# Three normalised groups turned by DMA as planes of 16-bit halves, and the first products begun by halves

## The reference

```
x = x + 0.5 * ffn(layernorm(x))
x = x + attention(layernorm(x))          # attention normalises again inside, with ln_w and ln_b
x = x + 0.5 * ffn(layernorm(x))

ffn(x):    logits = x @ gate_w.T + gate_b        # 8 experts
           g = top value of softmax(rms(logits) * rms_w / 0.5);  norm_g = g / (g + 1e-6)
           h = gelu(x @ w1[e] + b1[e])           # every expert, 256 hidden each
           out = norm_g * sum over e of (h @ w2[e] + b2[e])
attention: q, k, v = split(ln(x) @ w_qkv)        # 8 heads of 8
           q, k divided by their lengths;  softmax(8 * q @ k.T, causal) @ v;  @ w_out
```

## Time and profile before

| | |
|---|---|
| median of 3 runs | 269.8 us |
| the profiled execution | 269.82 us |
| its span, first to last instruction | 268.1 us |
| granted PE clock, mean | 0.998 |
| PE busy | 258.2 us |
| ACT busy | 217.5 us |
| DVE busy | 216.2 us |
| POOL busy | 80.7 us |

### The profile page before, as it was taken

One profiled execution on the slowest core, in us unless ns is written; L12 is line 12 of the kernel. 1 busy time (PEld: TensorE's weight loads), 2 busy tenths in 40 slices (PEclk: granted clock), 3 DMA queues, 4 the chain that ended last, 5 costly groups with the idle time before them and its releaser, 6 DMA issues.

```text
span 268.1 us, 5428 instructions
## 1 busy us (share of the span) xinstructions
PE 258.2 (96%) x1829; PEld 183.6 (69%) x1829; DVE 216.2 (81%) x590; ACT 217.5 (81%) x344; POOL 80.7 (30%) x175
## 2 busy tenths in 40 slices
PE   7999999999999999979998999999999999999995
PEld 6886878888788786533434433378888887888783
DVE  7999899998898987797378587378889678697784
ACT  2897668859878889999999999987777867859673
POOL 6302104204850482664349545520200000200100
PEclk9999999999999999999999999999999999999999
DMA  5741200001012104101314003300004211210311
GB/s 152 219 123 23 58 1 2 0 1 39 2 34 46 42 2 78 40 1 22 62 39 82 2 4 78 80 1 4 0 8 111 42 39 39 39 34 9 80 39 39
DMA packets 33343, 11.51 MB, mean 43 GB/s; under 512 B 24130, under 2 KB 32548, under 8 KB 33316
## 3 DMA queue, kind: packets, MB, share of 16 engines
q1 hardware_dynamic: 33172, 11.11, 17.7%
q10 hardware_dynamic: 144, 0.07, 0.1%
HBM read 4.88 MB, written 2.62 MB: 28 GB/s over the span
## 4 chain that ended last, share of the span: by engine, by line
PE 73%; DVE 8%; ACT 7%; issue 5%; POOL 4%; DMA 2%; SPq 0%; POOLq 0%; DVEq 0%; ACTq 0%
PE ps L590 10%; PE ps L596 10%; PE ps L608 10%; PE ps L593 10%; PE ps L613 10%; PE ps L611 9%; PE ps L746 5%; ACT probs L937 3%; PE ps L708 2%; PE ps L777 2%; ACT h L924 2%; POOL probs L1533 1%; POOL w_raw L1527 1%; DMA kT<-k_stack 1%; DVE h_lo L1100 1%
## 5 line engine op out<-in xcount | busy, mean ns | idle before, releaser
L924 ACT ACTIVATE h<-ps,cols 128x512 f32<-128x512 f32 x128 | 88.0, 694 | 36.2 <-PE ps L596 32.6
L1100 DVE TENSOR_TENSOR h_lo<-h,h_hi 128x512 fp32r<-128x512 f32 x128 | 88.6, 698 | 19.1 <-ACT h_hi L927 16.7
L937 ACT ACTIVATE probs<-ps 128x1024 f32<-128x1024 f32 (+1 forms) x80 | 65.0, 918 | 1.5 <-PE ps L708 1.4
L590 PE MATMUL ps<-xT_hi,w_hi 128*128 128x512 f32 x128 | 51.5, 402 | 0.0
L608 PE MATMUL ps<-h_hi,w_hi 128*128 128x512 f32 x128 | 50.5, 395 | 0.3 <-ACT yT L949 0.3
L927 ACT ACTIVATE h_hi<-ps,cols 128x512 fp32r<-128x512 f32 x73 | 50.2, 688 | 0.0
L613 PE MATMUL ps<-h_lo,w_hi 128*128 128x512 f32 x128 | 50.2, 392 | 0.0
L596 PE MATMUL ps<-xT_lo,w_hi 128*128 128x512 f32 x128 | 49.9, 390 | 0.0
L593 PE MATMUL ps<-xT_hi,w_lo 128*128 128x512 f32 x128 | 49.9, 390 | 0.0
L611 PE MATMUL ps<-h_hi,w_lo 128*128 128x512 f32 x128 | 49.9, 389 | 0.0
L746 PE MATMUL ps<-probs,v_ones 128*32 128x512 f32 (+4 forms) x384 | 34.2, 458 | 0.9 <-POOL probs L1533 0.6
(11 more groups left out here) (141 smaller groups left out, 273.2 us busy)
## 6 DMA issues: line engine op xcount, KB each, us to landing
w_raw<-in_L_ffn_w SPq DMA_DIRECT2D x8, 256.0 KB, 4.6
turned<-blocks SPq DMA_DIRECT2D x6, 256.0 KB, 2.0
w_raw<-turned SPq DMA_DIRECT2D x24, 64.0 KB, 2.3
w_raw<-v_ones SPq DMA_DIRECT2D x8, 128.0 KB, 2.4
x_sb<-in_L_attn_x SPq DMA_DIRECT2D x3, 256.0 KB, 6.8
out_x<-x_sb SPq DMA_DIRECT2D x3, 256.0 KB, 2.3
w_raw<-o_scaled SPq DMA_DIRECT2D x2, 256.0 KB, 4.3
x_sb<-in_L_attn_x SPq DMA_DIRECT2D x2, 128.0 KB, 2.3
```

Source lines behind the costliest of these rows:

```text
L590: pe.matmul(bank, w1_hi[:, w], xT_hi[:, cols_g], start=True, stop=False)
L924: first = nc.scalar.activation(h[:, slot, :], ps[:, BANK_H + slot, :], ACT.Gelu, bias=bias)
L937: nc.scalar.activation(probs[:, s % P_SLOTS, :, 0:width], ps[:, bank:bank + 2, 0:width], ACT.Exp, scale=SCALE).then_inc(exp_done, 1)
L1100: dve.tensor_tensor(h_lo[:, slot, :], h[:, slot, :], h_hi[:, slot, :].bitcast(f32), ALU.subtract).then_inc(split_done, 1)
```

## The change

Two u16 buffers `planes` and `planes_t` (128 x 2 x 512), `landed` (128 x 512), and semaphores. POOL copies the low and high 16-bit halves of a normalised group into two planes, SP turns both by one DMA transpose, and POOL puts the halves together again. Plane turn 0 is FFN group 3, turn 1 the attention norm of the last group, turn 2 FFN group 4. The PE transposes of these three and the jobs "ln" and "ffn_ln" go. In the start, two of the `keep_busy` calls go and the first pass of the first three chunks is split.

```
+            def turn_planes(n):                                   # SP
+                sp.wait_ge(planes_done, n + 1)
+                sp.dma_start_transpose(planes_t[...], planes[...]).then_inc(planes_in[n], 16)
+                if p == 0:
+                    turn_planes(0)                    # behind group 0's v corners
+                if p == LAST - 1:
+                    sp.wait_ge(xf_done[FFN], GROUPS)
+                    turn_planes(1)                    # ahead of group 2's stacks
+            sp.wait_ge(joined, 1)
+            turn_planes(2)                            # behind all stacks

+            def make_planes(n, kind, normed):                     # POOL
+                pool.wait_ge(xn_done[kind], GROUP_TILES * normed + GROUP_TILES)
+                if n:
+                    pool.wait_ge(planes_in[n - 1], 16)
+                words = xn[:, kind, :, :].rearrange("p t d -> p (t d)")
+                pool.tensor_copy(planes[:, :, :], by_plane(words)).then_inc(planes_done, 1)
+            def join_planes(n, words):
+                pool.wait_ge(planes_in[n], 16)
+                return pool.tensor_copy(by_plane(words), planes_t[:, :, :])
```

POOL's order in the first feed-forward part:

```
+                if layer == 0 and g == 2:
+                    make_planes(0, FFN, LAST)
+                    inverse_lengths(pool, 0, range(1))
+                    ln_twice(1)
...
+                    join_planes(0, xf[:, FFN, :]).then_inc(xf_done[FFN], 1)
+                    gate_root(2)
+                    inverse_lengths(pool, 0, range(1, 3))
+                    unit_vectors(pool, 0)
+                if layer == 0 and last:
+                    low_parts(pool, 0)
+                    inverse_lengths(pool, 1)
+                    ln_twice(2)
+                    unit_vectors(pool, 1)
+                    low_parts(pool, 1)
+                    gate_root(3)
```

and in the attention, behind the masks of the step named:

```
+                if s == 2 * last_quad[1] + 1:         # quad 5
+                    make_planes(1, ATT, LAST)
                 if s == 2 * last_quad[2] + 1:         # quad 12
+                    join_planes(1, landed[:, :]).then_inc(joined, 1)
                     ln_once(GROUPS)
                 if s == 2 * last_quad[5] + 1:         # quad 25
-                    gate_root(GROUPS)
+                    make_planes(2, FFN, GROUPS)
...
+                    join_planes(2, xf[:, FFN, :]).then_inc(xf_done[FFN], 1)
                     ln_once(GROUPS + 1)
                 if s == 2 * last_quad[6] + 1:
+                    gate_root(GROUPS)
```

Who uses them: ACT makes group 3's high part at chunk 10 and DVE its low part at chunk 11 of group 2 (before, 5 and 7). The high parts of the q and k stacks of groups 0 and 1 are made by ACT in chunks 0 and 9 of the last group (before, chunk 9 of group 2 and chunk 8 of the last). Jobs, gate and DVE:

```
-        jobs = [(q1, "ln", LAST), (q1 + 2, "project", (0, 0)), (q1 + 4, "project", (0, 1)),
-                (q1 + 5, "qkv", 0), (q1 + 7, "qkv", 1), (q2 + 3, "ffn_ln", 0),
+        jobs = [(q1 + 2, "project", (0, 0)), (q1 + 4, "project", (0, 1)),
+                (q1 + 5, "qkv", 0), (q1 + 7, "qkv", 1),
-        gate_at = {q2 + 4: GROUPS, quad_steps - 3: GROUPS + 1}
+        gate_at = {q3 + 1: GROUPS, quad_steps - 3: GROUPS + 1}
                 if kind == "qkv":                     # PE, fill
+                    pe.wait_ge(xf_done[ATT], GROUPS)
                 if (kind, arg) == ("project", (0, 1)):            # DVE
                     dve.wait_ge(job_emptied, n + 1)
                     first_stats(GROUPS)
+                    dve.wait_ge(joined, 1)
+                    dve.wait_ge(qkv_mm, LAST)
+                    dve.tensor_scalar(xf[:, ATT, :], landed[:, :], ...).then_inc(xf_done[ATT], 1)
                 if (kind, arg) == ("project", (1, 1)):
                     dve.wait_ge(job_emptied, n + 1)
                     first_stats(GROUPS + 1)
+                    dve.wait_ge(xf_done[FFN], GROUPS + 1)
+                    dve.tensor_copy(xT_hi[:, 0:GROUP], xf[:, FFN, :]).then_inc(early_hi, 1)
...
+                    low_features(dve, GROUPS)
+                    gate_logits(GROUPS, job_bank(n))
```

`gate_shift` and `gate_weight` of group 4 move behind DVE's last job, and their tanh on ACT from step 62 to 72. The start on PE:

```
+            def up_first_halves():
+                pe.wait_ge(first_half_hi, 1)
+                pe.wait_ge(w1_hi_ready, 1)
+                for c in range(LAG):
+                    pe.matmul(ps[:, BANK_H + c, 0:GROUP // 2], w1_hi[:, P * c:P * c + P], xT_hi[:, 0:GROUP // 2], start=True, stop=False)
             first_transposes(0, first_half_t)
-            keep_busy(2)
+            up_first_halves()
             first_transposes(1, ln_t[FFN])
...
-            keep_busy(2)
             for c in range(LAG):
                 up(0, 0, c, 0)                        # its first pass has 256 columns for these three
```

More of the change, by code:

```diff
@@ L189, in build @@
         blocks = sb("blocks", [P, GROUP])
+        u16 = mybir.dt.uint16
+        planes = sb("planes", [P, 2, GROUP], u16)
+        planes_t = sb("planes_t", [P, 2, GROUP], u16)
+        landed = sb("landed", [P, GROUP])
         turned_dram = [nc.dram_tensor(f"turned{n}", (P, GROUP), f32, kind="Internal").ap() for n in range(TURNS)]
@@ L232, in build @@
         o_zero = sem("o_zero")
+        planes_done, joined = sem("planes_done"), sem("joined")
+        planes_in = [sem(f"planes_in{n}") for n in range(3)]
         job_filled, job_emptied = sem("job_filled"), sem("job_emptied")
@@ L589, in up @@
                     pe.wait_ge(w1_hi_ready, c // 4 + 1)
-                pe.matmul(bank, w1_hi[:, w], xT_hi[:, cols_g], start=True, stop=False)
+                if n < LAG:
+                    pe.matmul(bank[:, GROUP // 2:], w1_hi[:, w], xT_hi[:, GROUP // 2:GROUP], start=False, stop=False)
+                else:
+                    pe.matmul(bank, w1_hi[:, w], xT_hi[:, cols_g], start=True, stop=False)
                 if starts:
@@ L596, in up @@
                 pe.matmul(bank, w1_hi[:, w], xT_lo[:, cols_g], start=False, stop=True).then_inc(up_done, 1)
+            def up_first_halves():
+                pe.wait_ge(first_half_hi, 1)
+                pe.wait_ge(w1_hi_ready, 1)
+                for c in range(LAG):
+                    pe.matmul(ps[:, BANK_H + c, 0:GROUP // 2], w1_hi[:, P * c:P * c + P], xT_hi[:, 0:GROUP // 2],
+                              start=True, stop=False)
             def down(layer, F, c):
@@ L653, in ffn_group @@
                         gate_product(F)
-                    if operands and c == at["ln_transpose"] and not last:
+                    if operands and c == at["ln_transpose"] and F + 1 < LAST:
                         if not first:
@@ L763, in fill @@
                 tiles = [slice(P * i, P * i + P) for i in range(GROUP_TILES)]
[L764 to L769, removed]
+                if kind == "qkv":
+                    pe.wait_ge(xf_done[ATT], GROUPS)
                     for i in halves[arg]:
@@ L978, in ffn_group @@
                             copy_qkv(g - 2)
-                        if c == at["qk_high"]:
-                            high_stacks(g - 2)
+                        if last and c == at["first_high"]:
+                            high_stacks(0)
+                        if last and c == at["qk_high"]:
+                            high_stacks(1)
                     if operands and 1 <= g < LAST and c == at["att_copy"]:
@@ L1397, in _ @@
                     first_stats(GROUPS)
+                    dve.wait_ge(joined, 1)
+                    dve.wait_ge(qkv_mm, LAST)
+                    dve.tensor_scalar(xf[:, ATT, :], landed[:, :], cols[:, COL_LNW:COL_LNW + 1], cols[:, COL_LNB:COL_LNB + 1],
+                                      ALU.mult, ALU.add).then_inc(xf_done[ATT], 1)
                 if (kind, arg) == ("qkv", 1):
@@ L1479, in ffn_group @@
                     ln_once(2 * GROUPS - 1)
-                if third:
-                    low_parts(pool, g - 2)
-                if layer == 0 and g == 1:
-                    ln_twice(g - 1)
-                    ln_once(F + 2)
             pool.memset(ones[:, :], 1.0).then_inc(const_self, 1)
```

73 lines of the change are left out of this document (37 added, 36 removed).

## The result

The changed kernel takes 272.99 us (median of 6 runs, 272.12 to 274.49) against 269.78 (6 runs, 269.74 to 269.87): ratio 1.0126, 95% interval 1.0092 to 1.0161. It is slower, as forecast, but by 3.2 us and not by 1.2, at the very edge of the range that was given. Its runs also spread over 2.4 us where those of the kernel before spread over 0.13. The profiled execution took 274.38 us (span 272.6), at the upper end of the spread; what follows reads it as such.

A forecast was written before the change was run, and what follows sets the result against it. PE was taken to bind the feed-forward part and ACT's exponentials the attention. Terms -0.25 + 0.3 + 0 + 1.25 - 0.5 + 0.4 = +1.2 on 269.8 gave 271.0 us, range 269.0 to 273.0.

The forecast's parts named there:

- Rival 2: POOL's copies run at two-input pace or are blocked by DVE, 2.0 us or more: 273.2 us, chance 0.13.
- qkv(0), +1.25: Attention: PE waits before qkv(0) for DVE's late xf, delaying scores and exponentials; +1.25 us, bounds +1.0 and +2.4.
- The removed "ln" job: Attention norm of group 3: removing PE's transposes and DVE's copy gives nothing back, as PE meets ACT again at 123.4; 0.
- Start, -0.25: First products: halves save 0.34 us and missing dummies up to 0.25, partly taken back by DVE; -0.25, bounds 0 and 0.6 gained.
- the granted clock would fall from 1.00: Sign at the start: expected in the first stretches if PE were granted less clock because the dummies are gone.
- Third group, +0.3: Feed-forward group 3: removed transposes give -0.39, PE's wait for late low parts costs 0.7; net +0.3, bounds -0.2 and +1.3.
- 0 for the last group: Last feed-forward group: stack copies landing in its first chunk fill ACT slack; 0, up to +0.4 if slack is used up.
- Removal of group 4's job, -0.5: Attention, near 149 us: transposes, PE's wait for DVE and two DVE copies go; -0.5 us, bounds -0.6 and 0.
- Gate product, +0.4: Attention, near 157 us: PE waits for group 4's joined planes, ACT has about 0.2 of lead; +0.4, bounds 0 and +3.5.
- The rule that I had quoted: A DVE instruction with two SBUF inputs and a GpSimd instruction reading SBUF exclude each other for the whole instruction.

The follow-up runs named there:

- e5: Changed kernel with its dummies back, POOL's join of the attention norm three masks earlier and DVE's xf ahead of group 4's statistics: 271.48 us, ratio 1.0065.
- e2: Kernel before without its four dummy matmuls, nothing else: 269.92 us (12 runs, 269.4 to 271.49), ratio 1.0011.
- e15: The changed kernel run again, unaltered: 273.39 us, ratio 1.0129, runs at 272.78, 273.01, 273.77 and 277.0.
- e1: Changed kernel with the four dummy matmuls put back, everything else of the change kept: 272.77 us, ratio 1.0111.
- e3: Kernel before with the whole start part (first passes by halves, no dummies) and nothing else: 269.72 us (269.45 to 271.73), ratio 1.0007.
- e7: On e1, group 3's features turned on PE again, with the earlier chunk numbers and POOL order: 271.39 us, ratio 1.0061.
- e11: On e1, DVE makes the low part of group 3's features in chunk 10 instead of 11: 271.54 us, ratio 1.0061.
- e12: On e10, group 3's features by planes, low part in chunk 10, POOL's unit vectors ahead of the attention norm's root: 269.81 us, ratio 1.0003.
- e10: Kernel before plus the attention's two plane turns, e5's join and xf, group 4's gate product two quads later, its DVE passes behind project(2,0): 269.69 us, ratio 0.9993.
- e9: On e1 with e5's and e7's edits and group 4's planes sooner, DVE reads gate rows ahead of cast and low part: 270.26 us, ratio 1.0014.
- e13: The kernel of e12 run once more: 269.51 us (10 runs, 269.18 to 271.25), ratio 1.0009.

## Why the prediction was right or wrong

The direction came out, and the main mechanism where and as large as forecast. The size failed: the sum of +1.2 lacks 2.0 us, in three of its terms: the start, the third group with the last, and the gate product. Rival 2's 273.2 is nearest to the measured time, but by luck: it rested on POOL copies of 2.0 us and more.

- **qkv(0), +1.25: right.** Wait 1.03 us, released by DVE's xf, 1.07 later behind it; e5 takes it away and gets 1.29. The chain was as written: masks until 131.9, join until 133.3, statistics until 133.6, xf. The removed "ln" job gave nothing, as written: PE is 0.6 us less late at 121.9 and has lost it again at 123.5. Planes took 1.04 us and joins 1.36 to 1.37 where I had 1.25 (and 1.54 in the estimate for a tight loop), so rival 2 is out; beside DVE one join took 1.88.
- **Start, -0.25: wrong in sign, and the step I had named as what could go wrong.** The dummies were costed as time, 0.25 us saved. Only the two at 7.34 were counted, and not the two at 5.69 that fill PE's wait there. They keep PE working: without them PE is at the lower clock for 3 us more (e2), or stays there from its first matmul to 14.0 us (changed kernel). In the median of the changed kernel that is +0.2 (e15 against e1); the start of the profiled run costs +2.05. In the runs of e2 and e3 that keep full pace the term is nearly right (269.56 against 269.75). The halves are not what saves: e2 without them is as quick as e3. I had said that the granted clock would fall from 1.00 if so; in the profile it did not, and only the distance between passes shows it.
- **Third group, +0.3, and 0 for the last group: mis-sized, 1.0 to 1.2 together in the timelines and 1.4 in the medians (e7).** The transposes gave their 0.41. The wait was put at 0.7 and is 0.85 in the changed kernel and 1.03 in e1, with PE's restart. The planes of turn 0 landed after 4.99 us and not 3.3, but in e1 they landed after 3.3 and the wait is no shorter; DVE's order decides (e11). What the forecast missed is the last group, +0.5: I had counted two stack copies on ACT as filling slack. It was not their length but their start, for POOL's unit vectors had moved behind the root of the attention norm and POOL's wait for its input; e12 puts them ahead and the loss is gone. I had followed POOL's new order only as far as the join.
- **Removal of group 4's job, -0.5: right in size.** The table shows -0.67, e10 about 0.7. It pays only as far as nothing behind it takes it back: in e10 0.2 goes where scores wait for ACT and 0.2 at the moved gate product.
- **Gate product, +0.4: half of it.** Its wait is 0.39. Behind it project(2,0) waits for the gate rows, which stand on DVE behind a cast and a low part (e9). The prediction saw DVE wait there and put the consequences at 0, having asked for the features' turn but not for the bank's next user. Together about +1.0.
- **Contention.** The rule that I had quoted (the Trainium skill, SBUF — State Buffer, Who interferes with whom) agrees with the trace: h_lo, with two inputs, takes 2.39 us for two beside the join, against 1.29 for two in e1 where the join had just ended. But the cast at 70.04, with one input, takes 1.07 beside the planes copy, and the one at 73.79 of e1 takes 1.58 beside the join, against about 0.4 elsewhere. The same section names copies and casts too, in their faster modes; I had counted only two-input passes.

For the median: 1.38 (e7) + 1.29 (e5) + 0.34 left for turn 2 and the halves = 3.0 (e1), and 0.2 for the missing dummies.

## What to carry to other kernels

When an instruction is moved behind another on one engine, follow every later instruction of that engine to whoever waits for it, up to the next place with slack. Here the joins were watched and the unit vectors and gate rows cost as much. Work taken off the busiest engine is worth its length only where that engine is the bound (0.41 in the feed-forward group, 0.13 in the attention). Dummy matmuls at a start are priced by the clock that they bring or hold, not by the time they fill, and over many runs, since one profile shows one kind of run.

## What the hardware showed unexpectedly

- The record of the granted clock stayed at 1.00 while PE ran at half pace from its first matmul to 14.0 us, in the profiled runs of the result and of e15; in e2 the same distance between passes comes with 0.50. The Trainium skill (TensorE: Matmul & The Clock Gate, Seeing it yourself) warns that such records can't be trusted one by one. Here the distance between equal passes (0.43 or 0.23 us) tells the pace.
- With the same 18 dummy records at the start, the full pace came at 4.4 us (before), 4.8 (e2), 6.8 (e1) or 14.0 us (changed kernel) in the profiled runs.
- A POOL copy of 1024 16-bit words took 1.04 us, the joining one 1.34 to 1.37 in most cases and 1.56 to 1.88 in six of the nine third groups.
- The DMA transpose of kT that lands in 3.2 us took 4.4, 5.0 and 5.1 us in three profiles (e12, e13, e15), with its issue on SP stretched from 1.33 to 2.3 to 2.6 us, each time with a 16 KB transfer of the instruction queue beside it.
